# Two biases moved from TensorE matmuls into a kept copy of x, with new queue orders, in a two-layer cross-attention and feed-forward kernel

## The chip, the cores and the metric

The kernel runs on one core of one Trainium2 chip. The metric is the device time of one execution in microseconds. A core has TensorE (PE in the profile, PEld its weight loads), VectorE (DVE), ScalarE (ACT), GpSimd (POOL) and SyncE (SP), which issues the DMA transfers. Each engine works through its own instructions in program order and waits on semaphores.

## The reference

x and ctx are 128 sequences of 128 rows of 256 numbers, in fp32. Cut to what matters here:

```
# layer 0: attention of x on ctx, 16 heads of 16
x  = x + (softmax(norm(x) Wq' + bq , ctx Wk' + bk) (ctx Wv' + bv)) Wo' + bo
# then two experts of eight, mixed by a gate
x  = x + sum_i gate_i * expert_i(norm(x))
# layer 1: attention with one 16x16 matrix shared by all heads, with a mask
x  = x + attn(norm(x), ctx, mask) Wo' + bo
# then a spiking feed-forward part: relu, square, projection, spike count
x  = x + spikes(norm(x)) / 5
```

The rows of a softmax sum to 1, so b_v adds the same row b_v Wo' to every output of the attention. The first attention's whole additive row is thus b_v Wo' + b_o; the second's is its bo.

## The kernel before

The program has four stages, one after the other: attention of layer 0, experts, attention of layer 1, spiking part. Both attentions are written by `attention`, with `first` true or false. A unit is a pair of sequences; there are 64 units. All steps of a unit are spread over about ten rounds of a software pipeline: `run_steps(eng, tasks, units, DEPTH)` goes, on each engine by itself, through rounds s = 0, 1, 2, ..., and in each through a list of tasks `(lag, task)`, doing the task for unit s - lag. The order of these lists and the lags were written out by hand for PE, ScalarE, VectorE, GpSimd and SyncE. "Step" below is the time from one round to the next.

What a unit goes through, in both attentions:

- SyncE loads x (`load_x`, into `xin`, two buffers) and ctx (`load_c`). VectorE takes the statistics of x, GpSimd finishes them and writes normalized x (`norm0`), PE transposes it (`t_x`), ScalarE and VectorE write the transposed block as a high and a low fp16 part (`hi_x`, `lo_x`). Every product of such values takes three passes (`three_passes`, L178 to L180).
- First attention: ctx is transposed (`t_c`, `hi_c`, `lo_c` into four buffers `cT`), then q, k and v are projected. `project_rows` makes v and, later, the attention's output o; each has 2 x 6 matmuls of 256 columns and 2 more (L713) that add the bias, by a matrix of constants times a row of the bias. In the second attention q is one folded product, ctx itself serves as k and as v, and only o goes through `project_rows`.
- q and k go to scratch in HBM (`store_q`, `store_k`) and come back in another layout with six transfers each (`stack_q`, `stack_k`, into `qS` and `kS`, four buffers). ctx's parts are stored for the second attention (`store_ct`), and `hi_c` waits, before it writes a `cT` buffer again, that the store of four units ago has landed.
- Scores are made twice: `score(0..3)` for the row maxima on VectorE (`row_max`, L988), and transposed, `score_t(0..3)`, for the exponentials on ScalarE (`expo`, L909). Row maxima go as three fp16 parts from GpSimd (`maxima`) by PE (`t_max`), ScalarE (`copy_max`) and two transfers (`store_max`, `place_max`) into `qS`. Score matmuls work on halves of the rows of PE. The second attention adds its mask with matmuls of 512 columns before each.
- `av(0..3)` multiplies by v in column groups of 32, `copy_y`, `y0`, `y1`, `norm_y` and `t_y` bring the result to o. SyncE loads x again (`reload_x` into `xr`), because `xin` has long been overwritten, and VectorE adds it to o (`add_x`). The sum is stored (`store_x1`), normalized again (`norm1`), transposed (`t_1`) and stored (`store_h`); the first attention also makes the gate's logits (`gate`).

Three PSUM banks (`ring3`) are shared by twelve products in the order of `plan`; `free` waits for the reader of the bank's product before. SyncE's list before, first attention:

```
tasks = [(5, store_max), (3, store_k), (3, stack_q), (3, stack_k), (5, place_max), (2, store_q),
         (0, load_x), (9, store_x1), (10, store_h), (0, load_c), (7, reload_x), (2, store_ct)]
```

`prepare_weights` splits weights and bias rows ahead of the first attention; `place_rows` copies each bias row into its buffer with two small transfers, one bias after the other.

## Time and profile before

| | us |
|---|---|
| median of 3 runs | 4155.69 |
| lowest and highest | 4152.24, 4157.76 |
| the profiled execution | 4155.79 |
| its span, first to last instruction | 4153.7 |
| mean granted TensorE clock | 0.974 |

A row of a timeline is: start in us from the span's start, duration in us, engine, line, operation, output<-inputs, shape, count of merged instructions, and in brackets the idle time of the engine before it and what ended it. "Issue" there means that the profile shows nothing that ended the wait. Durations of matmuls include their way through the array, so matmuls in a row overlap, and the distance between two starts tells what one costs.

### The profile page before, as it was taken

To read this page: it belongs to the slowest core of one execution; us is meant where nothing else is said; L and a number is where in the kernel's file an instruction comes from. 1 tells how busy PE (TensorE), PEld (TensorE's weight loads), DVE (VectorE), ACT (ScalarE), POOL (GpSimd) and SP (SyncE) were. 2 spreads that over 40 slices of the span, in tenths; PEclk is the share of its full clock that TensorE was granted. 3 is DMA by queue.
4 is the path that set the end of the run, shared out by engine and by line. 5 is a ranking of instruction groups with operands and counts; after the bars stand their busy time and mean duration, and the time that the engine had idled before them with its cause. 6 is when DMAs were issued, how large, how long until landed. Compare 5 with 4: busy or idle time off the path is not lost. (4 is left out here: it accounts for less than half of the span.)

```text
span 4153.7 us, 136312 instructions
## 1 busy us (share of the span) xinstructions
PE 3893.8 (94%) x48897; PEld 3072.9 (74%) x49084; DVE 2902.0 (70%) x5150; ACT 2205.9 (53%) x4610; POOL 1400.6 (34%) x2391
## 2 busy tenths in 40 slices
PE   5999999999299999999999997899999998999999
PEld 4777777777177777777777775566666666888888
DVE  4888888887655555555555555788888885777777
ACT  2666666666444444444444443566666665555554
POOL 4434433342200000000000001555555544777776
PEclk9999999999599999999999998899999999999999
DMA  4666666665611111111111111566666652222222
GB/s 120 186 197 189 192 195 195 184 199 160 207 39 40 38 35 40 38 38 37 39 39 35 40 38 53 154 184 186 187 186 184 186 171 80 74 75 74 77 77 72
DMA packets 627895, 471.77 MB, mean 114 GB/s; under 512 B 50592, under 2 KB 591342, under 8 KB 627262
## 3 DMA queue, kind: packets, MB, share of 16 engines
q1 hardware_dynamic: 625806, 462.68, 37.5%
q8 instruction: 432, 7.08, 0.7%
q14 instruction: 201, 1.65, 0.1%
q0 software_dynamic: 1456, 0.36, 0.0%
HBM read 291.91 MB, written 170.92 MB: 111 GB/s over the span
## 5 line engine op out<-in xcount | busy, mean ns | idle before, releaser
L1247 ACT ACTIVATE phase_loop_hf<-phase_loop_hid,phase_b1T 128x128 f32<-128x128 f32 x2048 | 586.2, 368 | 822.1 <-PE phase_loop_hid L180 821.9
L178 PE MATMUL phase_loop_hid<-phase_loop_moe_h,phase_w_hi 128*128 128x128 f16 x4096 | 734.5, 220 | 59.0 <-DMA phase_loop_moe_h<-h_scratch 58.8
L180 PE MATMUL phase_loop_hid<-phase_loop_moe_h,phase_w_lo 128*128 128x128 f16 x4096 | 732.0, 219 | 0.0
L179 PE MATMUL phase_loop_hid<-phase_loop_moe_h,phase_w_hi 128*128 128x128 f16 x4096 | 731.9, 219 | 0.0
L988 DVE TENSOR_REDUCE phase_loop_mx<-phase_loop_score 128x8 f32<-128x1024 f32 x512 | 622.7, 1216 | 123.4 <-PE phase_loop_score L743 115.7
L1215 PE MATMUL phase_loop_moe_y<-phase_w,phase_loop_hh 128*128 x2048 | 693.8, 379 | 0.2
L909 ACT ACTIVATE phase_loop_pt<-phase_loop_scoreT 128x1024 f32<-128x1024 f32 x512 | 524.1, 1024 | 280.4 <-PE phase_loop_scoreT L776 280.1
L1260 DVE TENSOR_SCALAR phase_loop_hh<-phase_loop_hf 128x512 f16<-128x512 f32 x512 | 217.7, 425 | 588.3 <-ACT phase_loop_hf L1247 307.0
L1217 PE MATMUL phase_loop_moe_y<-phase_w,phase_loop_hl 128*128 x2048 | 558.2, 273 | 0.0
L608 POOL MEMSET phase_loop_m<- 128x256 f16 x4 | 1.2, 312 | 1495.9 <-POOLq L167 1474.7
L178 PEld LDWEIGHTS phase_loop_hid<-phase_loop_moe_h,phase_w_hi 128*128 x4096 | 400.6, 98 | 111.8 <-issue 59.8
L179 PEld LDWEIGHTS phase_loop_hid<-phase_loop_moe_h,phase_w_hi 128*128 x4096 | 401.8, 98 | 5.6
L180 PEld LDWEIGHTS phase_loop_hid<-phase_loop_moe_h,phase_w_lo 128*128 x4096 | 400.7, 98 | 1.6
L1539 POOL TENSOR_TENSOR phase_loop_sp_q<-phase_loop_sp_r 128x512 f32<-128x512 f32 x256 | 330.9, 1293 | 157.3 <-ACT phase_loop_sp_r L1510 157.3
L1263 DVE SCALAR_TENSOR_TENSOR phase_loop_hl<-phase_loop_hf,phase_loop_hh 128x512 f16<-128x512 f32 x512 | 354.6, 693 | 17.6
L1215 PEld LDWEIGHTS phase_loop_moe_y<-phase_w,phase_loop_hh 128*128 128x128 f16 x2048 | 200.2, 98 | 187.1 <-issue 1.2
L804 PE MATMUL phase_loop_av<-phase_loop_pt,phase_loop_vx 128*32 128x128 f32 x8192 | 331.0, 279 | 4.5 <-ACT phase_loop_yE L917 2.0
L1563 DVE SCALAR_TENSOR_TENSOR phase_loop_sp_cnt<-phase_loop_sp_y,phase_loop_sp_cnt 128x512 f32<-128x512 f32 x256 | 320.6, 1252 | 8.8
L1510 ACT ACTIVATE phase_loop_sp_r<-phase_loop_sp_hid 128x512 f32<-128x512 f32 x256 | 153.0, 598 | 314.3 <-PE phase_loop_sp_hid L180 304.7
L178 PE MATMUL phase_loop_sp_hid<-phase_loop_sp_h,all_wf_hi 128*128 128x256 f16 x1024 | 280.0, 273 | 8.0 <-DMA phase_loop_sp_h<-h_scratch 8.0
L1494 PE MATMUL phase_loop_sp_yb<-all_wp_hi,phase_loop_sp_fh 128*128 128x256 f16 x1024 | 279.1, 273 | 1.3 <-POOL phase_loop_sp_fl L1445 1.3
L180 PE MATMUL phase_loop_sp_hid<-phase_loop_sp_h,all_wf_lo 128*128 128x256 f16 x1024 | 280.0, 273 | 0.0
(257 smaller groups left out, 9443.2 us busy)
## 6 DMA issues: line engine op xcount, KB each, us to landing
qk_scratch<-phase_loop_qk SPq DMA_DIRECT2D x192, 256.0 KB, 3.1
phase_loop_qS<-qk_scratch SPq DMA_DIRECT2D x768, 64.0 KB, 2.6
phase_loop_cin<-in_ctx SPq DMA_DIRECT2D x128, 256.0 KB, 4.5
x_scratch<-phase_loop_x SPq DMA_DIRECT2D x128, 256.0 KB, 3.5
h_scratch<-phase_loop_hT SPq DMA_DIRECT2D x128, 256.0 KB, 3.3
phase_loop_kS<-qk_scratch SPq DMA_DIRECT2D x384, 64.0 KB, 2.6
phase_loop_kS<-ct_scratch SPq DMA_DIRECT2D x384, 64.0 KB, 2.5
phase_loop_xin<-in_x SPq DMA_DIRECT2D x64, 256.0 KB, 3.2
```

What stands on the lines that cost most here:

```text
L178: eng.matmul(out, l_hi, r_hi, start=start, stop=False)
L179: eng.matmul(out, l_hi, r_lo, start=False, stop=False)
L180: return eng.matmul(out, l_lo, r_hi, start=False, stop=stop)
L804: m = pe.matmul(av_bank[32 * j:32 * j + 32, ch * S:(ch + 1) * S], vx[u.slot4][:, a, 2 * b + hh, :], pt[n % 2][:, hh * CH + j, :], start=Tr ...
L909: act.activation(pt[n % 2][:, :, :], score_t_bank[:, :].rearrange("p (j n) -> p j n", j=HB2), ACT.Exp, scale=exp_scale).then_inc(s_e.sem, 1)
L988: v.tensor_reduce(to, score_bank[:, :].rearrange("p (h j n) -> p h j n", h=2, j=CH), AX.X, ALU.max).then_inc(s_mx.sem, 1)
L1215: pe.matmul(o[:, :], hh[n % NH][:, j, :], row, start=half == 0 and j == 0, stop=False, skip_group_check=True)
L1217: m = pe.matmul(o[:, 0:D], hl[n % NH][:, j, :], row[:, 0:D], start=False, stop=False, skip_group_check=True)
L1247: i = act.activation(hf[n % NH][:, j, :], hid_bank[n % 4][:, j * S:(j + 1) * S], ACT.Gelu, bias=w["b1"][:, bass.ds(e * HB + (4 * half + j) ...
L1263: v.scalar_tensor_tensor(out=hl[n % NH][:, :, :], in0=hf[n % NH][:, :, :], scalar=p2(H_X), in1=hh[n % NH][:, :, :], op0=ALU.mult, op1=ALU. ...
L1539: g.tensor_tensor(q[n][:, :, :], r[n][:, :, :], r[n][:, :, :], ALU.mult).then_inc(s_q.sem, 1)
L1563: v.scalar_tensor_tensor(out=cnt[n % 2][:, :, :], in0=yy, scalar=at_least[n], in1=cnt[(n - 1) % 2][:, :, :], op0=ALU.is_ge, op1=ALU.add).t ...
```

## The change

- `bv` and `bo` leave the matmuls: `project_rows` has no bias any more. For the first attention a new `output_bias` computes b_v Wo' + b_o once, into `bo_b` on all 128 partitions; for the second `bo_b` is b_o.
- x stays in a ring of ten buffers from its load to `add_x`. A new task on GpSimd, `bias_x`, adds `bo_b` to it in place, after the normalization has read it. `reload_x` and `xr` are gone.
- The lists of all five engines and the banks' sharing are laid anew, in both attentions.

```diff
+def output_bias(kk, w, io, ready):
+    column, given = kk.sb("bv_column", [P, KB, 1], F32), kk.sb("bo_rows", [P, D], F32)
...
+        for kb in range(KB):
+            m = three_passes(pe, bank[:, 0:D], hi[:, kb, :], lo[:, kb, :], w["wo"][0][:, kb, :], w["wo"][1][:, kb, :],
+                             kb == 0, kb == KB - 1)
...
+        v.wait_ge(s_pe, 1)
+        v.scalar_tensor_tensor(out=w["bo_b"][:, :], in0=bank[:, 0:D], scalar=p2(-Y_X - W_X), in1=given[:, :],
+                               op0=ALU.mult, op1=ALU.add)
...
+    NX = 10
-        xin = two("xin", [P, PAIR, D], F32)
+        xin = [k.sb(f"xin{i}", [P, PAIR, D], F32) for i in range(NX)]
-        xr = two("xr", [P, PAIR, D], F32)
...
-            plan = [[(2, "q"), (6, "y0"), (1, "t_c")], [(2, "k"), (10, "gate"), (4, "t_max")],
-                    [(1, "t_x"), (6, "y1"), (2, "v")], [(6, "t_y"), (9, "t_1"), (7, "o")]]
-            shared = (("t_c", "t_max", "t_x", "t_y"), ("y0", "k", "y1", "o"), ("q", "gate", "v", "t_1"))
+            plan = [(10, "t_1"), (7, "y1"), (3, "v"), (8, "o"), (2, "t_x"), (7, "t_y"), (10, "gate"), (2, "q"),
+                    (1, "t_c"), (6, "y0"), (2, "k"), (4, "t_max")]
+            shared = (("t_1", "t_x", "y0", "t_max"), ("y1", "v", "t_y", "t_c"), ("o", "gate", "q", "k"))
...
                 def load_x(u):
                     ln0.s_xn.wait(sp, u.back(2))
-                    d_x.inc(sp.dma_start(xin[u.slot][:, :, :], xv[u.no]), u)
+                    s_x1.wait(sp, u.back(NX))
+                    d_x.inc(sp.dma_start(u.of(xin)[:, :, :], xv[u.no]), u)
-                def reload_x(u):
-                    s_x1.wait(sp, u.back(2))
-                    d_xr.inc(sp.dma_start(xr[u.slot][:, :, :], xv[u.no]), u)
...
                 if first:
-                    tasks = [(5, store_max), (3, store_k), (3, stack_q), (3, stack_k), (5, place_max), (2, store_q),
-                             (0, load_x), (9, store_x1), (10, store_h), (0, load_c), (7, reload_x), (2, store_ct)]
+                    tasks = [(0, load_x), (0, load_c), (8, store_x1), (4, store_max), (2, store_k), (2, stack_q),
+                             (4, place_max), (2, stack_k), (4, store_ct), (9, store_h), (1, store_q)]
                 else:
-                    tasks = [(5, store_max), (3, stack_q), (0, load_x), (5, place_max), (7, reload_x), (2, stack_k),
-                             (10, store_h), (2, store_q), (1, load_c), (8, store_x1)]
+                    tasks = [(9, store_x1), (4, load_c), (0, load_x), (5, store_max), (3, stack_q), (5, place_max),
+                             (10, store_h), (2, store_q), (2, stack_k)]
...
+                def bias_x(u):
+                    ln0.s_xn.wait(p, u)
+                    settle(p, ticks_g)
+                    x = u.of(xin)[:, :, :]
+                    p.tensor_tensor(x, x, w["bo_b"][:, :].unsqueeze(1).to_broadcast([P, PAIR, D]),
+                                    ALU.add).then_inc(s_xb.sem, 1)
                 if first:
-                    tasks = [(0, norm0), (3, maxima), (7, rstd1)]
+                    tasks = [(9, rstd1), (2, norm0), (3, bias_x), (4, maxima)]
                 else:
-                    tasks = [(3, ctx_as_v), (1, norm0), (9, rstd1), (4, maxima)]
+                    tasks = [(7, bias_x), (3, norm0), (6, ctx_as_v), (6, maxima), (10, rstd1)]
...
-                            three_passes(pe, o, x[:, 0, kb, at], x[:, 1, kb, at], hi[:, kb, :], lo[:, kb, :],
-                                         kb == 0, False)
-                        m = pe.matmul(o, ones[:, 0:S], w[bias][:, :], start=False, stop=True)
+                            m = three_passes(pe, o, x[:, 0, kb, at], x[:, 1, kb, at], hi[:, kb, :], lo[:, kb, :],
+                                             kb == 0, kb == KB - 1)
...
                 if first:
-                    tasks = some(plan[0]) + [(6, av(3)), (3, score(0)), (5, score_t(0))] + some(plan[1])
-                    tasks += [(3, score(1)), (5, score_t(1)), (5, av(0))] + some(plan[2])
-                    tasks += [(3, score(2)), (5, score_t(2)), (5, av(1))] + some(plan[3])
-                    tasks += [(3, score(3)), (5, score_t(3)), (5, av(2))]
+                    tasks = [(4, score(0)), (6, av(0)), (10, make["t_1"]), (7, make["y1"]), (6, av(1)), (4, score(1)),
+                             (6, score_t(2)), (3, make["v"]), (4, score(2)), (8, make["o"]), (2, make["t_x"]),
+                             (7, make["t_y"]), (6, av(2)), (10, make["gate"]), (4, score(3)), (6, score_t(3)),
+                             (2, make["q"]), (1, make["t_c"]), (6, make["y0"]), (6, av(3)), (5, score_t(0)),
+                             (2, make["k"]), (4, make["t_max"]), (5, score_t(1))]
                 else:
...
+                    tasks = [(6, av(3)), (4, make["t_max"]), (7, make["t_y"]), (9, make["t_1"]), (5, mask_score_t(1)),
+                             (3, mask_score(1)), (5, score_t(1)), (3, score(1)), (5, av(0)), (1, make["q"]),
+                             (6, make["y1"]), (5, mask_score_t(2)), (3, mask_score(2)), (5, av(1)), (3, score(2)),
+                             (5, score_t(2)), (7, make["o"]), (3, mask_score(3)), (5, mask_score_t(3)), (3, score(3)),
+                             (5, score_t(3)), (5, av(2)), (0, make["t_x"]), (5, make["y0"]), (2, mask_score(0)),
+                             (4, mask_score_t(0)), (2, score(0)), (4, score_t(0))]
...
                 if first:
-                    tasks = [(2, hi_q), (1, hi_c), (5, expo(0)), (6, copy_y(1)), (2, hi_k), (4, copy_max), (10, copy_gate),
-                             (1, hi_x), (5, expo(1)), (2, copy_v), (5, expo(2)), (6, hi_y), (9, hi_h), (5, copy_y(0)),
-                             (5, expo(3)), (8, norm1)]
+                    tasks = [(2, hi_k), (4, copy_max), (5, expo(1)), (9, hi_h), (5, copy_y(0)), (5, expo(2)),
+                             (2, copy_v), (8, norm1), (1, hi_x), (6, hi_y), (9, copy_gate), (5, expo(3)), (1, hi_q),
+                             (5, copy_y(1)), (4, expo(0)), (0, hi_c)]
...
                 def add_x(u):
                     s_o.wait(v, u)
-                    d_xr.wait(v, u)
+                    s_xb.wait(v, u)
...
                 if first:
-                    tasks = [(2, lo_k), (3, row_max(1)), (6, norm_y(1)), (10, top), (1, lo_x), (0, norm0_stats),
-                             (3, row_max(2)), (6, lo_y), (9, lo_h), (7, add_x), (3, row_max(3)), (5, norm_y(0)), (1, lo_q),
-                             (0, lo_c), (2, row_max(0)), (7, norm1_stats)]
+                    tasks = [(4, row_max(2)), (8, add_x), (2, lo_x), (7, lo_y), (4, row_max(3)), (1, norm0_stats),
+                             (2, lo_q), (6, norm_y(0)), (8, norm1_stats), (10, top), (1, lo_c), (2, lo_k),
+                             (3, row_max(0)), (6, norm_y(1)), (3, row_max(1)), (9, lo_h)]
```

ScalarE's and VectorE's lists of the second attention are reordered too; what matters of them is said where it is used.

## Rows read from the trace of the kernel before

**Rows 1.** Table of stretches: us, busy us of each engine (instructions), granted clock, DMA share, GB/s

```profile
200.00:900.00 700.00, 661.05 (x10197) 539.46 (x10193) 570.45 (x1189) 470.47 (x775) 278.64 (x637) 0.99 0.67 194
2700.00:3350.00 650.00, 639.02 (x9045) 441.60 (x9182) 550.77 (x1040) 428.95 (x643) 344.89 (x792) 1.00 0.64 186
```

**Rows 2.** Instructions on the tile vx: durations min/median/max in ns, first and last start

```profile
L895 ACT ACTIVATE phase_loop_vx<-phase_loop_ring x64: 597/597/598, 42.7 to 1004.1; 128x512 f32<-128x512 f32 x64
```

**Rows 3.** Timeline of TensorE, first attention

```profile
598.10 0.40 PE L743 MATMUL phase_loop_score<-phase_loop_kS,phase_loop_qS 48*128 48x128 f16 x8 [1.24 <-issue]
...
607.99 0.27 PE L180 MATMUL phase_loop_ring<-phase_wo_hi,phase_loop_yT 128*128 128x256 f16 x1
608.10 0.27 PE L713 MATMUL phase_loop_ring<-phase_bo_rows,all_ones 128*128 128x256 f16 x1
608.30 0.40 PE L743 MATMUL phase_loop_score<-phase_loop_kS,phase_loop_qS 48*128 48x128 f16 x8
608.53 0.39 PE L776 MATMUL phase_loop_scoreT<-phase_loop_qS,phase_loop_kS 51*128 51x128 f16 x8
608.85 0.64 PE L804 MATMUL phase_loop_av<-phase_loop_pt,phase_loop_vx 128*32 128x128 f32 x16
609.43 0.28 PE L178 MATMUL phase_loop_ring<-phase_loop_xT,phase_wq_hi 128*128 128x256 f16 x1
...
628.58 0.40 PE L743 MATMUL phase_loop_score<-phase_loop_kS,phase_loop_qS 48*128 48x128 f16 x8 [1.61 <-issue]
...
631.14 0.27 PE L762 MATMUL phase_loop_ring<-all_ident,phase_loop_m 128*128 128x128 f16 x2
...
645.37 0.27 PE L762 MATMUL phase_loop_ring<-all_ident,phase_loop_m 128*128 128x128 f16 x2
```

**Rows 4.** Waits of TensorE from 200 to 900 us: us in total, times, longest

```profile
PE phase_loop_score L743 <- issue: 37.8, 32, 2.9
```

**Rows 5.** Timeline of VectorE, the low part of q

```profile
612.24 0.68 DVE L950 SCALAR_TENSOR_TENSOR phase_loop_qk<-phase_loop_ring,phase_loop_qk 128x512 f16<-128x512 f32 x1
```

**Rows 6.** Timeline of SyncE, from store_q to place_max

```profile
613.02 0.38 SPq L537 DMA_DIRECT2D qk_scratch<-phase_loop_qk  x1
...
617.42 0.51 SPq L530 DMA_DIRECT2D ct_scratch<-phase_loop_cT  x1
...
618.57 0.38 SPq L542 DMA_DIRECT2D qk_scratch<-phase_loop_qk  x1
619.04 4.32 SPq L553 DMA_DIRECT2D phase_loop_qS<-qk_scratch  x6
623.46 2.74 SPq L553 DMA_DIRECT2D phase_loop_kS<-qk_scratch  x6
626.25 0.62 SPq L584 DMA_DIRECT2D phase_loop_qS<-max_scratch  x2
```

**Rows 7.** Tile ct_scratch from 200 to 900 us: time from issue to landing

```profile
DMA to landing us min/median/max: 3.7/5.0/7.9
```

**Rows 8.** Tile h_scratch from 2700 to 3350 us: time from issue to landing

```profile
DMA to landing us min/median/max: 2.2/2.6/4.2
```

**Rows 9.** Timeline of TensorE, second attention

```profile
2999.86 0.66 PE L396 MATMUL phase_loop_ring<-all_ident,phase_loop_ln0b_xn 128*128 128x128 f32 x4
...
3008.96 0.39 PE L743 MATMUL phase_loop_score<-phase_loop_kS,phase_loop_qS 48*128 48x128 f16 x8
3009.40 0.64 PE L804 MATMUL phase_loop_av<-phase_loop_pt,phase_loop_vx 128*32 128x128 f32 x16
...
3012.99 0.66 PE L396 MATMUL phase_loop_ring<-all_ident,phase_loop_ln0b_xn 128*128 128x128 f32 x4
```

**Rows 10.** Groups by line: count, busy us, mean ns, idle before; GpSimd

```profile
L1539 POOL TENSOR_TENSOR phase_loop_sp_q<-phase_loop_sp_r 128x512 f32<-128x512 f32 x256 | 330.9, 1293 | 157.3 <-ACT phase_loop_sp_r L1510 157.3
...
L387 POOL TENSOR_SCALAR phase_loop_ln0b_xn<-phase_loop_xin,phase_loop_ln0b_mv,phase_loop_ln0b_rs 128x256 f32<-128x256 f32 x128 | 156.6, 1228 | 13.5 <-issue 13.0 <-POOL phase_loop_ln0b_rs L364 0.4
```

**Rows 11.** Timeline of SyncE in the preparation

```profile
19.54 1.22 SPq L287 DMA_DIRECT2D phase_bv_rows<-prep_bv_parts  x2
```

More of the change, by code:

```diff
@@ L77, in back, with of @@
         return Unit(self.base, self.off - lag)
+    def of(self, buffers):
+        return buffers[self.no % len(buffers)]
 class Sig:
@@ L313, in vector, with sync, tensor @@
                                    op1=ALU.subtract).then_inc(s_lo, 1)
-    return {"sync": sync, "tensor": tensor, "scalar": scalar, "vector": vector}, clear_rows, place_rows
+    return {"sync": sync, "tensor": tensor, "scalar": scalar, "vector": vector}, clear_rows, place_rows, (s_lo, count)
+def output_bias(kk, w, io, ready):
+    column, given = kk.sb("bv_column", [P, KB, 1], F32), kk.sb("bo_rows", [P, D], F32)
+    wide = kk.sb("bv_wide", [P, KB, P], F32)
+    hi, lo = kk.sb("bv_hi", [P, KB, P], F16), kk.sb("bv_lo", [P, KB, P], F16)
+    bank = kk.ps("bv_ps")
+    s_ld, s_v, s_pe = (kk.sem(f"bv_{x}") for x in ("ld", "v", "pe"))
+    def sync(sp):
+        sp.dma_start(column[:, :, :], io["L0_xattn_b_v"].rearrange("o (b p) -> p b o", p=P),
+                     allow_slow_non_contiguous=True).then_inc(s_ld, 16)
+        sp.dma_start(given[:, :], io["L0_xattn_b_o"].to_broadcast([P, D])).then_inc(s_ld, 16)
+    def tensor(pe):
+        s_lo, count = ready
+        pe.wait_ge(s_lo, count)
+        pe.wait_ge(s_v, 3)
+        for kb in range(KB):
+            m = three_passes(pe, bank[:, 0:D], hi[:, kb, :], lo[:, kb, :], w["wo"][0][:, kb, :], w["wo"][1][:, kb, :],
+                             kb == 0, kb == KB - 1)
+        m.then_inc(s_pe, 1)
+    def vector(v):
+        v.wait_ge(s_ld, 32)
+        v.tensor_copy(wide[:, :, :], column[:, :, :].to_broadcast([P, KB, P])).then_inc(s_v, 1)
+        v.wait_ge(s_v, 1)
+        v.tensor_scalar(hi[:, :, :], wide[:, :, :], p2(Y_X), None, ALU.mult).then_inc(s_v, 1)
+        v.wait_ge(s_v, 2)
+        v.scalar_tensor_tensor(out=lo[:, :, :], in0=wide[:, :, :], scalar=p2(Y_X), in1=hi[:, :, :], op0=ALU.mult,
+                               op1=ALU.subtract).then_inc(s_v, 1)
+        v.wait_ge(s_pe, 1)
+        v.scalar_tensor_tensor(out=w["bo_b"][:, :], in0=bank[:, 0:D], scalar=p2(-Y_X - W_X), in1=given[:, :],
+                               op0=ALU.mult, op1=ALU.add)
+    return {"sync": sync}, {"tensor": tensor, "vector": vector}
 class Norm:
@@ L469, in attention @@
         s_g, s_gl, s_g8, s_gt = g("s_g"), g("s_gl"), g("s_g8", PAIR), g("s_gt")
+        s_xb = g("s_xb")
         s_idx, s_idxd = k.sem("s_idx"), k.sem("s_idxd")
         if first:
[L473 to L478 removed]
+            plan = [(10, "t_1"), (7, "y1"), (3, "v"), (8, "o"), (2, "t_x"), (7, "t_y"), (10, "gate"), (2, "q"),
+                    (1, "t_c"), (6, "y0"), (2, "k"), (4, "t_max")]
+            shared = (("t_1", "t_x", "y0", "t_max"), ("y1", "v", "t_y", "t_c"), ("o", "gate", "q", "k"))
+        else:
+            plan = [(4, "t_max"), (7, "t_y"), (9, "t_1"), (1, "q"), (6, "y1"), (7, "o"), (0, "t_x"), (5, "y0")]
+            shared = (("t_max", "y1", "t_x"), ("t_y", "q", "o"), ("t_1", "y0"))
         read = {"y0": (s_yn, 1), "y1": (s_yn, 2), "t_y": (s_yl, 1), "o": (s_x1, 1), "t_max": (s_mte, 1),
@@ L484, in attention @@
         for i, products in enumerate(shared):
-            bank = Bank([(name, lag, *read[name]) for part in plan for lag, name in part if name in products], units)
+            bank = Bank([(name, lag, *read[name]) for lag, name in plan if name in products], units)
             for name in products:
@@ L645, in norm0 @@
                     s_tx.wait(p, u.back(2))
[L646 removed]
+                    ln0.apply(p, u, u.of(xin))
                     if u.static and u.no < len(kS):
@@ L701, in fold_q, with project_rows @@
                     m.then_inc(s_q.sem, 1)
-                def project_rows(u, bank, src, name, bias, ones):
+                def project_rows(u, bank, src, name):
                     hi, lo = w[name]
```

48 lines of the change are left out of this document (21 added, 27 removed).

## The prediction

> **What bounds the kernel now.** I read the table of stretches first [rows 1]: it shows TensorE (PE) busy 661 of 700 us in the first attention stage and 639 of 650 in the second, with VectorE at 570 and 551 and GpSimd at 279 and 345. The expert and the spiking stages are not touched by the change, so only the two attention stages can move. The pace comes next. In the first stage the copies of v stand 42.7 to 1004.1 us apart over 63 steps [rows 2], which is 15.26 us a step; in the second the same transposes of x start 13.13 us apart [rows 9], and there PE hardly waits.
>
> Then PE's own timeline [rows 3], where the distance between starts counts and not the 273 ns given as duration: two 256-column matmuls start 0.11 us apart (607.99, 608.10). A step of the first stage in which nothing waits takes 14.23 us (631.14 to 645.37). So 15.26 holds about 1 us of something else, and the wait table says what [rows 4]: 37.8 us in 32 waits of 46 steps stand in front of the first score block, 2.9 at the longest. "Issue" hides the releaser, but the code waits there for the stacked q and k, which come by DMA. After the longest of those waits PE also runs slower: the granted clock of this stretch is 0.99 [rows 1]. Waits of 0.82 us and a slower clock of some 0.15 make up the 1 us.
>
> **Why it waits.** It is a loop over two steps: score(0) at 598.10 to score(0) at 628.58, 30.48 us [rows 3], where the matmuls between alone would take 2 x 14.23 = 28.46. Followed round: score(0), then 11.33 us of PE work to q of the unit two further on (609.43); its high and low part on ScalarE and VectorE are done at 612.92 [rows 5]; SyncE issues store_q at 613.02, and in its fixed order come then load_x, store_x1, store_h, load_c, reload_x, store_ct, store_max, store_k, six transfers of q and six of k [rows 6], which end at 626.2; the last lands and PE goes on at 628.58. From store_q to score is 15.6 us, nearly all of it one queue's issue time.
>
> **The matmuls that go.** v and o each lose two bias matmuls of 256 columns in the first stage, o two in the second: 4 x 0.109 = 0.44 us and 2 x 0.109 = 0.22 us a step. By the 273 ns of the table it would be 2.5 times as much, but those durations overlap.
>
> **The new order on PE** costs something. Each change between full matmuls, the score matmuls on half the rows and the attention-by-v matmuls in 32 columns opens a gap: after the bias matmul at 608.10 the score block starts 0.20 us later and not 0.11, so 0.096 us, and the block at 608.53 takes 0.32 us where the one before it took 0.23 (another 0.09) [rows 3]. The order before has 12 such changes in a step. The new order of the first stage is score, av, t_1 y1, av, score score_t, v, score, o t_x t_y, av, gate, score score_t, q t_c y0, av, score_t, k t_max, score_t: 15 changes, 3 more, +0.29 us. In the second stage it is 12 before and after. The Trainium skill, TensorEngine Tiling (Array Packing), Key Properties, has the rule that changing the tiling mode drains TensorE; it names no price. By a free switch the floor would be 13.79, by the row it is 14.23 - 0.44 + 0.29 = 14.08 us; I take the row's.
>
> **What becomes of the queue loop.** In the new order q comes 8.6 us after score(0) of the unit two before: three av (0.58 each), four transposes (0.44), v and o (12 x 0.109 each), six score blocks (0.23), the gate (0.35) and eight switches outside the av. That is 2.7 less than 11.33. On SyncE store_h, reload_x and store_ct no longer stand between store_q and the stacked k, place_max (0.7 [rows 6]) does: three one-transfer issues of 0.5 and a gap of 0.1 each (617.42; 618.57 to 619.04 for the gap) less 0.7, some 1.0 us less. The loop shrinks from 30.5 to 26.8 us, under 2 x 14.08 = 28.16. The longest wait seen, 2.9 [rows 4], is less than the 3.4 us by which loop and matmuls drew apart, so this wait should go.
>
> **What is late next.** store_ct moves behind the stacked k and lags 4 units; hi_c still waits for the store of four units back. That makes a loop over one step: store_ct lands (L), hi_c 0.60 (as the copy of that size in [rows 2]), lo_c and lo_k 0.68 each and handovers (2.05 together [rows 5]), store_k, six of q, six of k (618.57 to 626.25, 7.7) and place_max 0.7 [rows 6], then store_ct again: L + 10.45 us. Today L is 3.7 to 7.9, median 5.0 [rows 7], but there it is issued behind load_c and reload_x. The nearest row for its new place is store_h of the second stage, also 256 KB and directly behind six stacked k: 2.2 to 4.2, median 2.6 [rows 8]. So the loop is 13.1 us, 14.7 at the worst of that row, and it reaches 14.08 at L = 3.6. ScalarE's chain (copy_y1, expo0, hi_c, hi_k, copy_max, then t_1) and VectorE's (lo_k, two row maxima, then score) close within 0.3 us of the step too. For all of this I leave 0.25 us of waits a step (bounds: none, and today's 1.0). Step 14.33; gain (15.26 - 14.33) x 63 = 58.6 us.
>
> **x kept and biased.** The add is a new GpSimd instruction over 128x512 fp32 in two stages. Nearest row: a GpSimd tensor_tensor of that size, 1.29 us [rows 10]; bounds are that and two of the 1.23 us operations on half as much, 2.5. It lies on GpSimd, at 40% and 53% of its time, reads x that has been normalized, and is wanted four steps later in the first stage (lag 3 against 8); in the second (lag 7 against 7) bias_x goes ahead of norm0 and then ctx_as_v, and by my count of the order t_x and add_x come over 2 us after they are due. Behind it on GpSimd stand the six small steps of maxima; in the first stage they wait for the last row maximum anyway. Cost 0. Without that cover it would be 1.3 us a step. The 20 or 21 issues of SyncE fill some 12 of 14.1 us; the reload's 256 KB a step less make transfers no longer.
>
> **Second stage.** 13.13 - 0.22 = 12.91. One av block waits 0.12 us more than its like (3008.96 to 3009.40 is 0.44, against 0.32 at 608.53) [rows 3, 9]; with both mask blocks moved ahead it need not. Bounds 0.22 and 0.34, I take 0.30: x 62 = 18.6 us. A new loop here, t_max to s3 to the last row maximum to maxima to t_max, closes at about the step, hence not the full 0.34.
>
> **Preparation.** Two bias rows fewer are placed, 1.2 us each [rows 11]; the product of b_v and W_o hides behind the placing of the other three. Bounds 0 and 2.5 (the new loads may take back what the placing gives), I take 2.0.
>
> **Sum** on the profiled execution's own 4155.8 us (span 4153.7 and 2.1 around it; the median of the three runs is 4155.7, the same): 4155.8 - 58.6 - 18.6 - 2.0 = 4076.6, say 4077 us.
>
> **Rivals.**
> 1. *Transfers still pin the first stage.* If L is 4.2 to 4.8, or if store_k and store_max land late (the new order waits for each some 5 us after its issue, which is today's median of ct_scratch), the step is 14.65 to 15.26: 4155.8 - 20.6 - (0 to 38) = 4097 to 4135 us. For: today's 5.0. Against: the quiet moment of the new place.
> 2. *Slower, by the store_ct loop.* From L = 5.3 the step is over 15.76 and costs more than the rest gives (63 x 0.5 = 31.5 us against 20.6, and 0.2% more). At L = 5.5 the step is 15.95: 4155.8 + 43 - 21 = 4178 us. For: L has been 7.9. Against: it needs a median above today's.
> 3. *No waits at all and free switches.* 13.79 us: 93 + 21 + 2 less, 4040 us. Against: the gaps at every switch of the trace.
> 4. *GpSimd's add holds VectorE up.* If VectorE stood still for those 1.3 us, 1.05 would be left after the slack of its chain, in both stages: (14.33 + 1.05 - 15.26) x 63 + (12.83 + 1.05 - 13.13) x 62 - 2 = +52, 4208 us; at 0.63 a step in place of 1.05 the gain is just eaten up (125 x 0.63 = 79), 4156 us. Against: in these stages VectorE's large operations read one operand from PSUM. The Trainium skill, GPSIMD Engine Reference, Key points, says that contention is with VectorE operations in a two-port mode or with two SBUF inputs; by that rule too this rival has little to hold. No row here shows the add itself.
>
> **Chances.** Forecast 0.62 (its own range 4058 to 4096: waits of 0 to 0.45 us a step left, the bounds of the second stage and of the preparation); rival 1 0.18; rival 2 0.06; rival 3 0.08; rival 4 0.06, of which 0.04 near no change and 0.02 above it. Faster by over 0.2% (8 us, about what a measurement of this kernel can tell) 0.62 + 0.18 + 0.08 = 0.88; within it 0.04; slower 0.06 + 0.02 = 0.08. The range 4046 to 4130 takes in all of the forecast, nearly all of rival 1 and a part of rival 3: 0.8.
>
> **What would show it.** Steps of the first stage 14.1 to 14.5 us apart; no wait over 0.5 us at the first score block; bias add 1.3 us; ct_scratch landing near 2.6 to 3.2; the second stage at 12.8 to 12.9 a step with PE starts 0.109 apart in o. I am wrong if hi_c waits for ct_scratch in most steps, if stacked k begins late because of store_k or store_max, or if VectorE's instructions have become longer.

## The result, and the profile after

| | before | after |
|---|---|---|
| median, us | 4155.98 | 4058.68 |
| lowest and highest | 4152.24, 4157.76 | 4058.14, 4064.05 |
| the profiled execution; its span | 4155.79; 4153.7 | 4064.05; 4062.1 |

The ratio is 0.977, with a 95% interval of 0.9753 to 0.9787: 97 us less, where 79 were forecast (4077 us, own range 4058 to 4096). The direction and the stages are as forecast; the median stands 0.7 us above the lower end of the range, so the gain was under-sized, by 18 us.

The table of stretches and the copies of v, which answer to [rows 1, 2]:

```profile
200.00:900.00 700.00, 698.85 (x10951) 564.09 (x10949) 631.11 (x1293) 514.90 (x847) 367.17 (x744) 1.00 0.65 193
2700.00:3350.00 650.00, 646.08 (x9308) 435.18 (x9306) 547.79 (x1044) 430.49 (x659) 398.68 (x843) 1.00 0.57 165
```

```profile
L941 ACT ACTIVATE phase_loop_vx<-phase_loop_ring x64: 597/597/599, 42.0 to 923.8; 128x512 f32<-128x512 f32 x64
```

TensorE is now busy 699 of 700 us in the first attention (661 before), and VectorE 631 (570). The step is 881.8 / 63 = 14.00 us, where it was 15.26. In TensorE's waits from 200 to 900 us the 37.8 us at the score block [rows 4] are gone; this is the only line that is left:

```profile
PE phase_loop_ring L436 <- ACT phase_loop_mT L948: 0.7, 2, 0.4
```

TensorE's timeline in the first attention (as [rows 3]) has one step from t_max (L807) to t_max, and within it the way from score(0) to q:

```profile
595.34 0.28 PE L807 MATMUL phase_loop_ring<-all_ident,phase_loop_m 128*128 128x128 f16 x2
...
595.78 0.39 PE L788 MATMUL phase_loop_score<-phase_loop_kS,phase_loop_qS 48*128 48x128 f16 x8
...
604.43 0.28 PE L181 MATMUL phase_loop_ring<-phase_loop_xT,phase_wq_hi 128*128 128x256 f16 x1
...
609.38 0.28 PE L807 MATMUL phase_loop_ring<-all_ident,phase_loop_m 128*128 128x128 f16 x2
...
623.87 0.39 PE L788 MATMUL phase_loop_score<-phase_loop_kS,phase_loop_qS 48*128 48x128 f16 x8
```

A step without a wait is 14.04 us, forecast 14.08. From score(0) to q it is 8.65 us, forecast 8.6. SyncE goes on from there (as [rows 6]):

```profile
607.59 0.36 SPq L575 DMA_DIRECT2D qk_scratch<-phase_loop_qk  x1
...
611.00 0.38 SPq L580 DMA_DIRECT2D qk_scratch<-phase_loop_qk  x1
611.47 2.96 SPq L591 DMA_DIRECT2D phase_loop_qS<-qk_scratch  x6
614.48 0.61 SPq L622 DMA_DIRECT2D phase_loop_qS<-max_scratch  x2
615.20 3.78 SPq L591 DMA_DIRECT2D phase_loop_kS<-qk_scratch  x6
619.09 0.38 SPq L568 DMA_DIRECT2D ct_scratch<-phase_loop_cT  x1
619.56 0.45 SPq L561 DMA_DIRECT2D h_scratch<-phase_loop_hT  x1
621.68 0.36 SPq L575 DMA_DIRECT2D qk_scratch<-phase_loop_qk  x1
```

The stacked k is issued by 618.98. With the 2.6 us that such a transfer takes (median of the tile qk_scratch) it is there at 621.6, and the score block that needs it runs at 623.87. The loop of two steps has become 25.8 us long inside 28.1, with 2.3 us to spare. SyncE stands idle for 1.7 us in front of the last store_q shown.

In the second attention the transposes of x start 12.81 us apart (13.13 before, [rows 9]):

```profile
3004.26 0.66 PE L436 MATMUL phase_loop_ring<-all_ident,phase_loop_ln0b_xn 128*128 128x128 f32 x4
...
3017.07 0.66 PE L436 MATMUL phase_loop_ring<-all_ident,phase_loop_ln0b_xn 128*128 128x128 f32 x4
```

By stages, profiled execution against profiled execution: preparation 24.9 to 23.3 us (-1.6); first attention, from the first load of x to the last store of h, 1033.4 to 954.8 (-78.6); from there to the store of the indices 3.7 to 2.2 (-1.5); second preparation 88.1 to 92.7 (+4.6); experts 1418.7 to 1418.5; second attention 893.3 to 879.0 (-14.4). Together these are the 91.7 us between the two executions. The second attention counts to its last stores. The other three runs of the kernel after are 5 to 6 us shorter than its profiled one; in which stage, no trace here shows.

### The profile page after: what moved, and what is told of

It reads as the page before. It is cut to its first block and busy times, and to the rows that moved or that the text cites. A ratio compares the mean times of both kernels' runs of the same rounds, so it can differ in the third digit from the quotient of the medians.

```text
span 4062.1 us, 135969 instructions
## 1 busy us (share of the span) xinstructions
PE 3863.0 (95%) x48706; PEld 3024.4 (74%) x48706; DVE 2905.5 (72%) x5151; ACT 2195.7 (54%) x4607; POOL 1572.2 (39%) x2515
## 5 line engine op out<-in xcount | busy, mean ns | idle before, releaser
L1586 POOL TENSOR_TENSOR phase_loop_sp_q<-phase_loop_sp_r 128x512 f32<-128x512 f32 x256 | 348.6, 1362 | 139.5 <-ACT phase_loop_sp_r L1557 139.5
L181 PE MATMUL phase_loop_sp_hid<-phase_loop_sp_h,all_wf_hi 128*128 128x256 f16 x1024 | 280.3, 274 | 7.5 <-DMA phase_loop_sp_h<-h_scratch 7.5
L182 PE MATMUL phase_loop_sp_hid<-phase_loop_sp_h,all_wf_hi 128*128 128x256 f16 x1024 | 280.2, 274 | 0.0
```

The lines of the kernel that those rows point to most:

```text
L181: eng.matmul(out, l_hi, r_hi, start=start, stop=False)
L182: eng.matmul(out, l_hi, r_lo, start=False, stop=False)
L1586: g.tensor_tensor(q[n][:, :, :], r[n][:, :, :], r[n][:, :, :], ALU.mult).then_inc(s_q.sem, 1)
```

## The experiments

The theory: in the old orders the loop of two steps through SyncE set the first attention, so matmuls and issues taken out of it give only their share by two. The new orders make it shorter than TensorE's own work, and only then does each matmul count in full. The main rival: the gain is the matmuls and the second load of x that went, and the orders add little.

The experiments are numbered e1 to e12 below. Each was measured with runs of the kernel before beside it (medians 4154.58 to 4155.43 us), and its ratio is against those; the intervals reach about 0.2%, 8 us, to either side. "More than after" compares medians with 4058.68 us, so a few us of such a difference mean nothing; steps and waits read from the traces are finer.

**The parts, each alone.** First the bias matmuls, left out of the kernel before (e1):

```diff
-                            three_passes(..., kb == 0, False)
-                        m = pe.matmul(o, ones[:, 0:S], w[bias][:, :], start=False, stop=True)
+                            m = three_passes(..., kb == 0, kb == KB - 1)
```

> The kernel before with the bias matmuls of v and o left out and nothing else changed (b_v and b_o are then missing from the output). Theory A, the queue loop of two steps sets the first stage: the loop holds v and o once, so 0.44 us in two steps, 0.22 us a step; with 0.22 us a step of the second stage 63 x 0.22 + 62 x 0.22 = 27.5 us less, about 4128 us. Rival, TensorE's matmuls alone set both stages: 63 x 0.44 + 62 x 0.22 = 41 us less, about 4114 us. Second rival, transfers pin the first stage whatever TensorE does: 14 us less, about 4142 us.

Measured: 4142.79 us, ratio 0.9974 (0.9961 to 0.9987), 11 us less; the profiled span is 15 us shorter. By the total alone the second rival (4142 us) would be right; the trace says otherwise. In it the copies of v go from 43.1 to 990.2 us, 15.03 a step, 14.3 us less in all: the theory's figure for the first attention. But the second attention gives next to nothing, its transposes start 13.11 us apart instead of 13.13. TensorE's waits of 2700 to 3250 us show why; here the kernel before, then this one:

```profile
PE phase_loop_av L804 <- ACT phase_loop_yE L917: 0.9, 3, 0.3
```

```profile
PE phase_loop_av L803 <- ACT phase_loop_yE L916: 11.3, 42, 0.5
```

One av block a step now waits 0.27 us for copy_y on ScalarE. The matmuls taken out came back as this wait. In the kernel before, the same block already started 0.12 us late [rows 9], which the view of waits put down in three cases only.

Then the ring alone (e2: x in ten buffers, `reload_x` gone from SyncE's lists, nothing else):

> The kernel before with x kept in the ring of ten buffers and the second load of x gone; bias matmuls and all orders as before. Theory A: SyncE has one issue (0.6 us with its gap) less in the loop of two steps, 0.3 us a step of the first stage, nothing in the second: 63 x 0.3 = 19 us less, about 4137 us. Rival, the kernel is bound by matmuls: no change, 4156 us. Second rival, the 256 KB less a step shorten every transfer and with them the loop further: more than 30 us less, under 4126 us.

Measured: 4124.64 us, ratio 0.9934 (0.9917 to 0.995), 27 us less by the ratio and 30 by the medians: more than the theory's 19, at the second rival's bound. The step is (971.5 - 43.2) / 63 = 14.74 us, 0.52 less and not 0.3, so the whole gain (63 x 0.52 = 33 us in the profiled execution) lies in the first attention. The issue was under-sized: from the start of reload_x to the next issue the trace of before has 0.81 us in the mean, not 0.6, which by the loop of two steps makes 0.40 a step; and the stores land sooner. Tile max_scratch from 200 to 850 us, before, then ring alone:

```profile
DMA to landing us min/median/max: 1.9/4.4/7.5
```

```profile
DMA to landing us min/median/max: 1.4/3.7/5.5
```

The granted clock from 200 to 900 us is 1.00 here and was 0.99. What the landings and what the clock have of the other 0.12 us was not separated.

All of the change but the orders (e3; of its edit, the place of the add in the first attention):

```diff
-                    tasks = [(0, norm0), (3, maxima), (7, rstd1)]
+                    tasks = [(0, norm0), (3, bias_x), (3, maxima), (7, rstd1)]
```

> The whole change without the new orders: ring, no bias matmuls, the add on GpSimd, with the lists of all five engines as before (the add goes in behind norm0, in the second stage behind rstd1). Theory A: the loop of two steps loses 0.44 + 0.6 us, 0.52 us a step, 33 us; the second stage 0.22 x 62 = 14; the preparation 2: 49 us less, about 4107 us, so about half of the change's 97 us is the orders'. Rival, the orders give nothing of their own: about 4059 us. Second rival, the add in the old order is waited for or holds VectorE up: over 4120 us.

Measured: 4109.22 us, ratio 0.9892 (0.9875 to 0.9908), 45 us less, for 49 forecast. So about half of the change's 97 us is the orders'. That the sum came out is in part luck, for its two main terms missed in opposite directions. The first attention's step is 14.63 us, 0.62 less and not 0.52 (39 us for 33); with the 0.81 us of e2 for the issue, (0.44 + 0.81) / 2 is 0.62. The second attention gave nothing for 14: its transposes still start 13.13 us apart, and the av block waits for copy_y, 12.1 us in 42 waits from 2700 to 3250 us, as in e1. Here the step swings. Timeline, t_max to t_max:

```profile
300.62 0.27 PE L807 MATMUL phase_loop_ring<-all_ident,phase_loop_m 128*128 128x128 f16 x2
...
314.41 0.27 PE L807 MATMUL phase_loop_ring<-all_ident,phase_loop_m 128*128 128x128 f16 x2
...
331.29 0.37 PE L807 MATMUL phase_loop_ring<-all_ident,phase_loop_m 128*128 128x128 f16 x2
```

13.79 us where nothing waits, 16.88 in the next step. 13.79 is 14.23 less 0.44, the floor with the old order. The new order's 14.04 is 0.25 above it, for three changes of the kind of matmul: 0.083 each, 0.096 was taken. The new order of TensorE is dearer by itself and pays because nothing waits in it.

The new orders and the ring, with the bias matmuls put back and no add on GpSimd (e4):

> The kernel after with the bias matmuls of v and o put back and the add on GpSimd gone (ring and new orders stay). Theory A, after the change TensorE's own work sets both stages: 63 x 0.44 + 62 x 0.22 + 2 of the preparation = 43 us more than after, about 4102 us. Rival, in the new order a transfer loop (store_ct) sets the first stage and hides matmuls: its 0.44 us a step costs nothing, only the second stage's 14 and the 2, about 4075 us.

Measured: 4100.81 us, ratio 0.9871 (0.9855 to 0.9888), 42 us more than after, as the theory has it. The steps without a wait are 14.48 (+0.43, expected 0.44) and 13.01 us (+0.20, expected 0.22). The same matmuls, four a step in the first attention and two in the second, were worth 11 us in the old orders and are worth some 40 in the new ones (63 x 0.43 + 62 x 0.20; the forecast has 2 more for the preparation).

e2 and e4 differ in the orders alone, and so do e3 and the kernel after. The orders are thus worth 24 us with the bias matmuls in (4124.64 to 4100.81) and 51 without them (4109.22 to 4058.68). Neither part has a price of its own: each is worth more with the other.

**The add on GpSimd.** e5: bias_x taken out of GpSimd's lists, and add_x's wait for it:

> The kernel after without the add of the biases on GpSimd (b_v Wo' and b_o are then missing from the output; x stays in the ring). Theory A, the add is covered: within 4 us of the kernel after, 4059 us. Rival, GpSimd's add holds VectorE or the shared memory up: up to 1 us a step in both attentions less, some 60 to 120 us, under 4000 us; a part of it, 0.1 us a step, would be 12 us.

Measured: 4060.8 us, ratio 0.9771 (0.9752 to 0.979), the same as after. The add is there and costs nothing: its group on GpSimd in the first attention of the kernel after (1272 ns, forecast 1290), then VectorE's row maxima in the kernel after and in the kernel without the add:

```profile
L695 POOL TENSOR_TENSOR phase_loop_xin<-phase_loop_xin,phase_bo_b 128x512 f32<-128x512 f32 x46 | 58.5, 1272 | 0.0
```

```profile
L1034 DVE TENSOR_REDUCE phase_loop_mx<-phase_loop_score x184: 1214/1216/1226, 202.5 to 843.8; 128x8 f32<-128x1024 f32 x184
```

```profile
L1033 DVE TENSOR_REDUCE phase_loop_mx<-phase_loop_score x185: 1212/1216/1226, 202.2 to 849.4; 128x8 f32<-128x1024 f32 x185
```

The Trainium skill, GPSIMD Engine Reference, Key points, names as the cases of contention between GpSimd and VectorE a VectorE instruction in a two-port mode or with two SBUF inputs. VectorE's large operations here have an operand in PSUM, and the trace agrees with that rule (1216 ns with the add and without it).

**SyncE's list.** e6: store_ct moved behind store_h and store_q:

```diff
-    (4, place_max), (2, stack_k), (4, store_ct), (9, store_h), (1, store_q)]
+    (4, place_max), (2, stack_k), (9, store_h), (1, store_q), (4, store_ct)]
```

> The kernel after with store_ct moved from behind the stacked k to the end of SyncE's list, behind store_h and store_q. Theory A, there is a loop of one step of L + 10.45 us that closes only a little under the step: two issues of some 0.55 us go into it, L + 11.55; at L = 2.9 that is 14.45, at L = 3.5 15.05 us, 0.4 to 1.0 us above today's 14.05: 25 to 63 us slower than after, 4084 to 4122 us. Rival, four cT buffers give it more than a microsecond of room: no change, 4059 us.

Measured: 4262.09 us, ratio 1.0252 (1.0226 to 1.0277), 203 us more than after and far outside what either theory gave. Copies of v from 41.5 to 1123.6 us, 17.18 a step. SyncE's timeline, then ScalarE's:

```profile
616.49 0.45 SPq L568 DMA_DIRECT2D ct_scratch<-phase_loop_cT  x1
...
630.64 0.38 SPq L561 DMA_DIRECT2D h_scratch<-phase_loop_hT  x1
632.24 0.38 SPq L575 DMA_DIRECT2D qk_scratch<-phase_loop_qk  x1
632.72 0.45 SPq L568 DMA_DIRECT2D ct_scratch<-phase_loop_cT  x1
```

```profile
619.67 0.60 ACT L918 ACTIVATE phase_loop_cT<-phase_loop_ring 128x512 f16<-128x512 f32 x1 [2.09 <-DMA ct_scratch<-phase_loop_cT]
...
630.82 0.60 ACT L929 ACTIVATE phase_loop_qk<-phase_loop_ring 128x512 f16<-128x512 f32 x1 [0.61 <-PE phase_loop_ring L735]
...
635.86 0.60 ACT L918 ACTIVATE phase_loop_cT<-phase_loop_ring 128x512 f16<-128x512 f32 x1 [2.06 <-DMA ct_scratch<-phase_loop_cT]
```

store_q does not only take 0.5 us to issue, it waits for q. So store_ct now inherits that wait, and the loop runs through TensorE's step: hi_c 619.67, then nearly a whole step of TensorE to hi_q 630.82 (11.15), store_q 632.24 (1.42), store_ct 632.72 (0.48), landing and hi_c 635.86 (3.14), together 16.19 us. From copy_max, which stands behind hi_c on ScalarE, the delay goes on to TensorE, which waits at t_1 in every step (waits from 200 to 850 us):

```profile
PE phase_loop_ring L436 <- ACT phase_loop_mT L948: 85.0, 38, 3.3
```

I had counted the issues of the queue that store_ct was moved past, and not what they wait for. The rest up to 17.18 goes with the granted clock, which is 0.93 from 200 to 900 us here and 1.00 in the kernel after. Most of the steps in which it is 1.00 take 16.2 us, those with less some 17.5 us or more. In one of these, behind a wait of 1.93 us at t_1, it fell for some 3 us to 0.51, the lower of its two levels (1.2 and not 2.4 GHz); the row has the columns of [rows 1]:

```profile
637.50:640.80 3.30, 3.30 (x38) 2.55 (x39) 2.13 (x5) 1.80 (x3) 3.15 (x3) 0.51 0.40 108
```

In that stretch an av block takes 1.02 us (start at 639.09, the next block's at 640.11) and not 0.58. A wait of 2.26 us at t_1 one step later left the clock at 1.00. The direction is the theory's (the place of store_ct sets the step when it closes late), the loop is another one.

SyncE's list of before in the first attention, all other lists new (e7):

```diff
-    tasks = [(0, load_x), (0, load_c), (8, store_x1), (4, store_max), (2, store_k), (2, stack_q),
-             (4, place_max), (2, stack_k), (4, store_ct), (9, store_h), (1, store_q)]
+    tasks = [(5, store_max), (3, store_k), (3, stack_q), (3, stack_k), (5, place_max), (2, store_q),
+             (0, load_x), (9, store_x1), (10, store_h), (0, load_c), (2, store_ct)]
```

> The kernel after with SyncE's list of before in the first attention (without the reload), all other lists new. Theory A, the loop store_q to score had 1.3 us of room after the change and the old list puts store_h and store_ct in (1.2 us) and takes place_max out (0.7 us): the step stays 14.0 to 14.3 us, 4059 to 4078 us. Rival, the order of SyncE's list gave the gain: the step goes back to the 14.64 us of the kernel with all but the orders, 4099 us. Second rival, maxima placed late under the old lags are waited for: over 14.64 us.

Measured: 4090.28 us, ratio 0.9838 (0.982 to 0.9856), 32 us more than after; 14.44 us a step, between the theory's and the rival's figures. The loop store_q to score is not what waits. TensorE's waits from 200 to 850 us have one line:

```profile
PE phase_loop_scoreT L821 <- DMA phase_loop_qS<-max_scratch: 19.6, 21, 1.7
```

It is the second rival's mechanism at a smaller size: the placed maxima are late, at every second step. So in the same list place_max alone was moved ahead of stack_k (e10):

```diff
-    tasks = [(5, store_max), (3, store_k), (3, stack_q), (3, stack_k), (5, place_max), (2, store_q),
+    tasks = [(5, store_max), (3, store_k), (3, stack_q), (5, place_max), (3, stack_k), (2, store_q),
```

> The same as the run with SyncE's old list in the new orders (4090 us, where TensorE waited at the first score_t block for the placed maxima, 19.6 us in 21 waits), with place_max alone moved ahead of stack_k. Theory A, of the whole new SyncE list only this move matters: the placed maxima come six issues (3.4 us) earlier, the waits go, and the step is 14.0 to 14.1 us: 4058 to 4066 us. Rival, the old list is late for another reason (store_h and store_ct between store_q and the stacked q and k, longer transfers): 4075 us or more.

Measured: 4056.75 us, ratio 0.9757 (0.9732 to 0.9781), not to be told from the kernel after. Its steps are 14.05 us, and the copies of v go from 41.9 to 917.3 us (13.90 a step over the whole stage, its beginning included). Of SyncE's new list, then, one move is needed. SyncE's timeline in e10, store_q and the stacked k of its unit:

```profile
601.57 0.38 SPq L575 DMA_DIRECT2D qk_scratch<-phase_loop_qk  x1
...
611.49 2.69 SPq L591 DMA_DIRECT2D phase_loop_kS<-qk_scratch  x6
```

That is 12.6 us where the new list takes 11.4 (607.59 to 618.98 above). With the other parts of the loop as in the kernel after it is some 27.0 us long, an estimate, still under 28.1. The prediction let the loop shrink by 2.7 us on TensorE and by 1.0 in the queue; the first is enough. Which of the other lists (TensorE's, ScalarE's, VectorE's, GpSimd's) and of the banks' sharing are needed was not separated, nor was SyncE's list of the second attention.

The second load of x, put back into the new orders (e8; add_x's wait for it is not shown):

```diff
+                def reload_x(u):
+                    s_x1.wait(sp, u.back(2))
+                    d_xr.inc(sp.dma_start(xr[u.slot][:, :, :], xv[u.no]), u)
...
-    tasks = [(0, load_x), (0, load_c), (8, store_x1), ...
+    tasks = [(0, load_x), (0, load_c), (7, reload_x), (8, store_x1), ...
...
-    tasks = [(9, store_x1), (4, load_c), (0, load_x), ...
+    tasks = [(9, store_x1), (4, load_c), (6, reload_x), (0, load_x), ...
```

> The kernel after with x loaded a second time as before (256 KB a step into two buffers that nobody reads; add_x waits for the load and adds the kept x), behind load_c in the first attention and in the second. It asks what the ring gives once the orders are new; in the old orders it gave 30 us. Theory A: SyncE stands waiting 1.4 us a step for store_max and 1.4 for store_q, the reload's 0.6 to 0.8 us of issue goes into the first of these waits: no change, 4055 to 4065 us. Rival, the transfers' time counts: landings as long as before (4.4 to 5.1 us for store_max, store_k) close the store_ct loop and the step goes up by 0.3 us or more: over 4078 us.

Measured: 4413.88 us, ratio 1.0613 (1.0586 to 1.064). The first attention alone answers the question: copies of v from 42.1 to 928.3 us, 14.07 a step against 14.00. In the first attention the ring's own gain is 33 us in the old orders (63 x 0.52) and 4 in the new (63 x 0.07). The 350 us are the second attention's and my placing. SyncE's timeline there:

```profile
3003.33 0.47 SPq L553 DMA_DIRECT2D phase_loop_cin<-in_ctx  x1
3012.37 0.36 SPq L566 DMA_DIRECT2D phase_loop_xr<-x_scratch  x1
...
3022.26 1.59 SPq L553 DMA_DIRECT2D phase_loop_cin<-in_ctx  x1
3030.34 0.36 SPq L566 DMA_DIRECT2D phase_loop_xr<-x_scratch  x1
```

reload_x waits until add_x of two units back has freed its buffer. At lag 6 that is the add of lag 8, and it stands at lag 7, late in VectorE's list: the queue stands 8.6 us in front of xr (3003.80 to 3012.37) with everything behind it late. TensorE waits for the stacked q (2700 to 3250 us):

```profile
PE phase_loop_score L793 <- DMA phase_loop_qS<-qk_scratch: 112.9, 30, 5.3
```

What the reload costs in the second attention in a fitting place was not measured.

**Fewer changes of kind on TensorE.** e9 (its third edit, an earlier load of b_o, is not shown):

```diff
-    tasks = [(4, score(0)), (6, av(0)), (10, make["t_1"]), (7, make["y1"]), (6, av(1)), ...
+    tasks = [(4, score(0)), (10, make["t_1"]), (7, make["y1"]), (6, av(0)), (6, av(1)), ...
-             ... (7, make["t_y"]), (6, av(2)), (10, make["gate"]), (4, score(3)), ...
+             ... (7, make["t_y"]), (10, make["gate"]), (6, av(2)), (4, score(3)), ...
...
-             ... (3, score(1)), (5, av(0)), (1, make["q"]), (6, make["y1"]), (5, mask_score_t(2)),
-             (3, mask_score(2)), (5, av(1)), ...
+             ... (3, score(1)), (1, make["q"]), (6, make["y1"]), (5, mask_score_t(2)),
+             (3, mask_score(2)), (5, av(0)), (5, av(1)), ...
```

> The kernel after with three cheap edits that leave the matmuls as they are: in the first attention t_1 and y1 stand ahead of av(0) and the gate ahead of av(2) (13 changes of the kind of matmul in a step where there were 15), in the second av(0) stands directly ahead of av(1) (11 for 12), and b_o of layer 1 is loaded ahead of the first attention and not in the second preparation. Theory A, each change of kind costs 0.096 us and TensorE sets both stages: 63 x 0.19 + 62 x 0.096 = 18 us less, and up to 4.6 us of the second preparation: 4036 to 4041 us; steps 13.86 and 12.54 us. Rival, the gaps at the changes hide something else or the moved blocks make ScalarE late: no change or slower, 4059 to 4080 us.

Measured: 4078.39 us, ratio 0.9812 (0.9794 to 0.9831), 20 us more than after. The second attention does what was said: 12.72 us a step where nothing waits, 0.09 less. In the first the step is 14.39, and TensorE has a new wait:

```profile
PE phase_loop_ring L437 <- ACT phase_loop_mT L949: 17.8, 45, 0.7
```

t_1 shares its bank with t_max. Moved one av block (0.58 us) ahead, it comes before copy_max has read the bank: 0.40 us a step. Without that move (e11):

> The kernel after with three edits of the run with fewer changes of kind, without the move of t_1 and y1 that made TensorE wait for copy_max (17.8 us in 45 waits): the gate ahead of av(2) in the first attention (14 changes for 15), av(0) next to av(1) in the second (11 for 12), b_o of layer 1 loaded ahead of the first attention. Theory A: 63 x 0.096 + 62 x 0.096 = 12 us less and 0 to 4.6 of the second preparation, 4042 to 4047 us, steps 13.90 and 12.54 us. Rival, the move of the gate costs as t_1 did: step of the first stage over 14.05 us, 4052 us or more.

Measured: 4063.39 us, ratio 0.9771 (0.9749 to 0.9792), no gain that these runs can tell: the median is 5 us above that of after, the profiled execution 0.7 us shorter. It is the rival's case. The second attention's step is again 12.72, but the first's is 14.10, 0.05 above that of after though one change of kind is gone. From t_y to score(3), kernel after, then this one:

```profile
602.33 0.60 PE L436 MATMUL phase_loop_ring<-all_ident,phase_loop_yn 128*128 128x128 f32 x4
602.86 0.65 PE L849 MATMUL phase_loop_av<-phase_loop_pt,phase_loop_vx 128*32 128x128 f32 x16
...
603.88 0.40 PE L788 MATMUL phase_loop_score<-phase_loop_kS,phase_loop_qS 48*128 48x128 f16 x8
```

```profile
404.93 0.60 PE L437 MATMUL phase_loop_ring<-all_ident,phase_loop_yn 128*128 128x128 f32 x4
405.53 0.17 PE L181 MATMUL phase_loop_ring<-phase_wg_hi,phase_loop_hT 128*128 128x8 f16 x1
...
405.95 0.64 PE L850 MATMUL phase_loop_av<-phase_loop_pt,phase_loop_vx 128*32 128x128 f32 x16
406.53 0.40 PE L789 MATMUL phase_loop_score<-phase_loop_kS,phase_loop_qS 48*128 48x128 f16 x8
```

1.55 us before, 1.60 now. Behind the fp32 transposes the gate's first matmul starts 0.60 us after t_y, where t_y itself takes 4 x 0.109 = 0.44: a gap of 0.16 without a change of kind, more than the 0.09 that the change cost. Nothing waits in the view. b_o's earlier load, the third edit, shows nothing: from the last store of h of the first attention to the second attention's first transposed x the kernel takes 1524.4 us here, 1524.6 with e10's list and 1525.7 in the kernel after.

And with av(2) of the second attention next to av(3) too (e12):

> As the run with the gate and the second stage's av(0) moved, and in the second attention av(2) too, from behind score_t(3) to the end of TensorE's list, next to av(3): 10 changes of kind for 12. Theory A: 62 x 0.096 = 6 us less again, 4036 to 4041 us, step of the second attention 12.44 us. Rival, expo(0) on ScalarE waits for av(2) (it writes the same buffer), ScalarE is late for the masks that follow and TensorE waits: step over 12.54 us, slower than without the move.

Measured: 4082.3 us, ratio 0.9816 (0.9795 to 0.9838), 19 us more than without the move; the step is 13.06. The rival was right. ScalarE's waits from 2700 to 3250 us, then TensorE's:

```profile
ACT phase_loop_pt L956 <- PE phase_loop_av L850: 77.4, 42, 2.1
```

```profile
PE phase_loop_ring L181 <- DVE phase_loop_yT L997: 13.0, 40, 0.5
```

expo(0) waits 1.84 us a step for av(2). What ScalarE does after it is late, hi_y among it, and lo_y on VectorE waits for that. TensorE in its turn waits at o for lo_y, and not at the masks that the rival named. The combination that these runs point to, e10's list with the second attention's av(0) moved and nothing else, would by 62 x 0.09 be some 6 us faster, an estimate and less than the intervals here can tell; it was not run.

## Why the prediction was right

The mechanism held, the two-step loop leaving TensorE's own matmuls as the limit; one term, the waits left over, was too large, and the median came out at the edge of the range. By part:

- *What bounds the kernel* held. The wait at the score block is gone; e1 and e3 show the loop's share by two, and e4 the full price once the loop is short.
- *The matmuls that go*: 0.43 and 0.20 us a step measured for 0.44 and 0.22. The term stands in the new orders only; in the old ones the second attention's part came back as a wait for copy_y (e1).
- *The new order on PE*: three more changes cost 0.25 us, forecast 0.29; floor 14.05 for 14.08.
- *The queue loop*: 8.65 us for 8.6 on TensorE. From q to store_q 3.16 for 3.59, and from store_q to the stacked k in place 14.0 for 14.6. In all 25.8 for 26.8. The part in the queue was not needed (e10): the shortening on TensorE alone brings the loop under two steps.
- *store_ct*: L was taken as 2.6. Tile ct_scratch from 200 to 850 us, as [rows 7]:

```profile
DMA to landing us min/median/max: 2.3/2.4/4.3
```

  The loop of L + 10.45 is 12.9 us at the median, and hi_c waited for it three times (1.1 us in all). This is also why the waits were overstated: **the 0.25 us a step left for waits is the term that was mis-sized.** In the steady part next to nothing is left (0.7 us from 200 to 900 us). 63 x 0.25 = 16 us, with 2 for the floor and 3 to 4 for a quicker beginning of the stage, is the difference between 58.6 forecast and 79 measured.
- *x kept and biased*: cost 0, as forecast (e5). The prediction counted on no shorter transfers from the ring; in the old orders they do get shorter (4.4 to 3.7 us for max_scratch), and e2 gave 0.52 us a step for it all, 0.40 of it by the issue.
- *The second stage*: 13.13 to 12.81, 0.32 for 0.30. The bigger half is the matmuls, 0.20; with them put back (e4) the orders alone give 0.11, about the av block's wait of 0.12. Over the whole stage 14.4 us came instead of 18.6. The 64 transposes of x take 17.4 us less from the first to the last (813.9 to 796.5); from the last of them to the end of the stage it takes 3 us longer.
- *Preparation*: 1.6 us for 2.0. Not foreseen: 4.6 us more in the second preparation. The expert weights' raw loads there take 75.4 us where they took 70.7. Why is open; the early load of b_o changed nothing. Part of it is no effect of the change: e1 and e2, with the second preparation of the kernel before, show 73.1 and 72.3 us for the same loads.
- The rivals: transfers pinning the first stage (1) and the store_ct loop (2) did not come, but each is one place in SyncE's list away: in e7 the placed maxima come late, in e6 store_ct sets the step, if by a longer loop than the forecast's L + 10.45. Free changes of kind (3) are refuted by 14.05 against 13.79, and the add holding VectorE up (4) by e5.

## What to carry to other kernels

What an instruction is worth depends on the loop that it lies in: the same bias matmuls were worth 11 us while a two-step loop or another engine's copy set the pace, and some 40 us once TensorE did. Take the length of every loop round its engines and queues, and compare it with the step, before an instruction is priced. When a transfer is moved in a queue, count what the entries that it is moved behind wait for, and what it waits for itself, not only issue times: leaving that out cost 200 us in e6 and 350 in e8, and a single entry moved the right way (place_max, e10) gave all that the new list of the first attention gave.

## What the runs showed of the hardware

- A change between full, half-row and 32-column matmuls costs 0.08 to 0.09 us each: 0.25 for three (e3 against after), 0.09 for one (e9). The Trainium skill, TensorEngine Tiling (Array Packing), Key Properties, says that such a change drains TensorE, without a price; the trace agrees. But a gap of 0.16 us also stands between fp32 transposes and the gate's 8-column fp16 matmuls, where the kind does not change (e11).
- The stretches with much idle time of TensorE have the lower granted clock: 1.00 in the first attention of the kernel after, with 1 us idle in 700, 0.99 in the kernel before with 39 and 0.93 in e6 with 91; in e8's second attention 0.87, with 113 us idle in 550 (2900 to 3450 us). In e6 such waits cost more than their length: a step of 16.2 us at 1.00 takes 17.5 or more when the clock falls to its lower level for some 3 us in it.
- An issue on SyncE is not of one price: in the kernel before it took 0.70 us in the mean for reload_x and 0.48 for store_h (0.81 and 0.52 to the start of the next issue, from 200 to 850 us).
